# A mixture-of-experts kernel on one core: 71 half tiles a unit in place of 72

## The reference

```python
def moe(t, router, W1, b1, W2, b2):          # t: 4096 tokens x 128 channels, one image
    weight, index = top_k(softmax(layernorm(t) @ router), 2)
    h = gelu(einsum("nd,edf->enf", xn, W1) + b1)     # 128 -> 512
    y = einsum("enf,efd->end", h, W2) + b2           # 512 -> 128
    return t + einsum("ne,end->nd", combine(weight, index), y)
x = x + gated(ln(x));      x = x + moe(x, layer 0)    # both images
x = x + pools(ln(x));      x = x + moe(x, layer 1)    # max pools of 7 sizes, mixed
```

## Time and profile before

| | us |
|---|---|
| median of 3 runs | 1134.44 |
| lowest, highest | 1126.28, 1143.79 |
| the profiled execution | 1131.95 |
| its span, from the first to the last instruction | 1130.2 |
| busy in it: PE, POOL, DVE, ACT | 832.7, 620.7, 566.2, 522.3 |

### The profile page before, as it was taken

How to read it: one execution, slowest core, us unless ns; L and a number is a source line. 1 busy time by engine, 2 the same in 40 slices (tenths; PEclk the granted TensorE clock), 3 DMA queues, 4 the chain that set the end, 5 groups by cost and what they waited for, 6 DMA issues and landing times.

```text
span 1130.2 us, 14753 instructions
## 1 busy us (share of the span) xinstructions
PE 832.7 (74%) x4305; PEld 701.0 (62%) x4305; DVE 566.2 (50%) x1308; ACT 522.3 (46%) x1427; POOL 620.7 (55%) x598
## 2 busy tenths in 40 slices
PE   1854389888977777986787579976886877778780
PEld 1434267776776665865777467866776755657680
DVE  8957902280500292999883577999481003300004
ACT  1405045453454445653294256642483534444463
POOL 1000266766766655688634555788545665656651
PEclk9876579988988877998689598987797987879895
DMA  7001343443465752454157633533255645636356
GB/s 315 1 0 65 128 144 116 138 134 111 157 210 187 231 191 89 148 158 131 42 153 249 229 120 110 184 119 97 69 137 195 209 154 163 204 113 213 113 182 223
DMA packets 55391, 167.63 MB, mean 148 GB/s; under 512 B 13888, under 2 KB 13901, under 8 KB 55056
## 3 DMA queue, kind: packets, MB, share of 16 engines
q1 hardware_dynamic: 36880, 130.98, 34.7%
q0 software_dynamic: 18432, 35.70, 11.2%
HBM read 137.26 MB, written 31.46 MB: 149 GB/s over the span
## 4 chain that ended last, share of the span: by engine, by line
PE 43%; DVE 23%; ACT 11%; issue 9%; another core or an unknown queue 9%; DMA 2%; POOL 1%; SPq 0%; POOLq 0%; ACTq 0%; DVEq 0%
PE h_ps L773 15%; PE yT_ps L786 14%; DVE state L1292 5%; PE turn_ps L708 5%; ACT hT L586 4%; DVE work L1278 4%; DVE work L1273 4%; PE acc_ps L725 3%; PE acc_ps L745 2%; DVE work L1286 2%; PE xT_ps L762 2%; ACT yT L597 1%; ACT work L624 1%; PE yr_ps L796 1%
## 5 line engine op out<-in xcount | busy, mean ns | idle before, releaser
L501 POOL DMA_INDIRECT xg<-xn_rows,tile_rows x288 | 307.7, 1068 | 247.1 <-DVEq L1208 126.7
L510 POOL DMA_INDIRECT y_rows<-yr,tile_rows x288 | 308.8, 1072 | 238.6 <-ACT yr L606 157.2
L773 PE MATMUL h_ps<-xT,expert 128*128 128x256 f32 (+1 forms) x1408 | 327.3, 382 | 76.6 <-issue 40.9
L786 PE MATMUL yT_ps<-hT,expert 128*128 128x256 f32 (+1 forms) x1408 | 310.6, 373 | 40.8 <-ACT yT L597 37.3
L586 ACT ACTIVATE hT<-h_ps,expert 128x256 f32<-128x256 f32 (+1 forms) x704 | 254.6, 449 | 153.5 <-PE h_ps L773 62.9
L773 PEld LDWEIGHTS h_ps<-xT,expert 128*128 128x128 f32 x1408 | 250.3, 214 | 116.4 <-issue 75.0
L786 PEld LDWEIGHTS yT_ps<-hT,expert 128*128 128x128 f32 x1408 | 254.6, 212 | 80.6 <-ACT yT L597 45.2
L1242 DVE SCALAR_TENSOR_TENSOR tok<-work,share,tok 128x128 f32<-128x128 f32 x224 | 61.5, 345 | 343.4 <-DMA work<-y_rows 341.4
L597 ACT ACTIVATE yT<-yT_ps,expert 128x256 f32<-128x256 f32 (+1 forms) x176 | 74.1, 443 | 188.0 <-PE yT_ps L786 87.3
L574 ACT ACTIVATE xT<-xT_ps 128x256 f32<-128x256 f32 x144 | 56.4, 392 | 97.5 <-PE xT_ps L762 64.7
L762 PE MATMUL xT_ps<-ident,xg 128*128 128x128 f32 x288 | 61.7, 298 | 40.3 <-DMA xg<-xn_rows,tile_rows 32.8
(11 more groups left out here) (210 smaller groups left out, 644.3 us busy)
## 6 DMA issues: line engine op xcount, KB each, us to landing
expert<-in_experts SPq DMA_DIRECT2D x176, 514.5 KB
work<-y_rows SPq DMA_DIRECT2D x24, 512.0 KB
xn_rows<-work SPq DMA_DIRECT2D x16, 512.0 KB, 5.0
xg<-xn_rows,tile_rows POOLq DMA_INDIRECT x288
y_rows<-yr,tile_rows POOLq DMA_INDIRECT x288
tok<-in_x_tokens SPq DMA_DIRECT2D x8, 512.0 KB, 7.0
state<-in_x SPq DMA_DIRECT2D x2, 2048.0 KB, 17.4
work<-y_rows SPq DMA_DIRECT2D x16, 256.0 KB, 6.0
```

Of the source, the lines that this page charges most:

```text
L501: pool.indirect_dma_start(xg[:, s, h, :], None, xn_rows[unit], bass.IndirectOffsetOnAxis(ap=tile_rows[unit % 2][:, at, 0, h:h + 1], axis=0)) \
L510: pool.indirect_dma_start(y_rows[unit], bass.IndirectOffsetOnAxis(ap=tile_rows[unit % 2][:, at, 1, h:h + 1], axis=0), yr[:, s, h, :], None ...
L773: mm = pe.matmul(h_ps[c // 2][:, c % 2, cols], expert[:, t.load(h) % W_RING, c * P:(c + 1) * P], xT[:, t.slot(2), cols], start=True, stop= ...
L786: mm = pe.matmul(yT_ps[:, cols], expert[:, t.load(h, d) % W_RING, HIDDEN + c * P:HIDDEN + (c + 1) * P], hT[:, s, c, cols], start=(c == 0), ...
```

## The change

The 72nd half tile is left out. A new constant `SEATS` = 71 counts the half tiles of a unit, and the last tile (tile 35) has one half in place of two. Its gather, `turn_x`, `turn_y` and scatter issue one instruction instead of two; its `up` and `down` have 4 matmuls of 128 columns each instead of 8; `activate` has four instructions instead of eight, and `copy_y` one instead of two. `copy_x` and `copy_rows` stay as they are, at 256 columns, and so do the tables of routing, which keep 72 columns, but for the list of experts, which has 43. `LOADS` is 43. `landed`, which gives the semaphore value to wait for, now leaves out the halves that the short tiles don't have.

```diff
-LOADS = FULL + SPLIT * HALVES
+SEATS = (PAIRS + EXPERTS * (P - 1)) // P
+LOADS = SEATS - FULL
...
-    def landed(self, d=0, each=1):
-        return ((self.s + d) // RING + 1) * 16 * each
+    def landed(self, d=0):
+
+        at = self.s + d
+        short = sum(HALVES * TILES - SEATS for u in range(at // TILES + 1)
+                    if (u + 1) * TILES - 1 <= at and ((u + 1) * TILES - 1 - at) % RING == 0)
+        return ((at // RING + 1) * HALVES - short) * 16
+
+    def halves(self, d=0):
+
+        return min(HALVES, SEATS - HALVES * self.at(d)[1])
 
     def parts(self, d=0):
 
-        return HALVES if self.at(d)[1] >= FULL else 1
+        return self.halves(d) if self.at(d)[1] >= FULL else 1
...
     n = t.parts(d)
-    return [(h, slice(h * SLOTS // n, (h + 1) * SLOTS // n)) for h in range(n)]
+    size = t.halves(d) * P // n
+    return [(h, slice(h * size, (h + 1) * size)) for h in range(n)]
...
-                for h in range(HALVES):
+                for h in range(t.halves(d)):
                     pool.indirect_dma_start(xg[:, s, h, :], None, xn_rows[unit],
...
-                for h in range(HALVES):
+                for h in range(t.halves(d)):
                     pool.indirect_dma_start(y_rows[unit],
...
-                for h in range(HALVES):
+                for h in range(t.halves(d)):
                     mm = pe.transpose(xT_ps[:, h * P:(h + 1) * P], xg[:, t.slot(RING, d), h, :], ident[:])
...
-                for h in range(HALVES):
+                for h in range(t.halves(d)):
                     mm = pe.transpose(yr_ps[:, h, :], yT[:, s, h * P:(h + 1) * P], ident[:])
```

More of the change, by code:

```diff
@@ L426, in load_outputs @@
                     for d in range(RING):
-                        sp.wait_ge(s_scat[last.slot(RING, -d)], last.landed(-d, HALVES))
+                        sp.wait_ge(s_scat[last.slot(RING, -d)], last.landed(-d))
                     sp.wait_ge(s_buf, u + 1)
@@ L603, in copy_rows @@
                 if t.old(d - RING):
-                    act.wait_ge(s_scat[s], t.landed(d - RING, HALVES))
+                    act.wait_ge(s_scat[s], t.landed(d - RING))
                 act.wait_ge(s_yr_ps, t.done(d))
@@ L757, in turn_x @@
             def turn_x(t, d):
-                pe.wait_ge(s_gath[t.slot(RING, d)], t.landed(d, HALVES))
+                pe.wait_ge(s_gath[t.slot(RING, d)], t.landed(d))
                 if t.old(d - 1):
                     pe.wait_ge(s_xt_sb, t.done(d - 1))
-                for h in range(HALVES):
+                for h in range(t.halves(d)):
                     mm = pe.transpose(xT_ps[:, h * P:(h + 1) * P], xg[:, t.slot(RING, d), h, :], ident[:])
```

## The result

The changed kernel takes 1124.64 us (median of 11 runs, 1117.01 to 1131.13) against 1133.34 for the kernel before in the same runs. The ratio is 0.9906, 95% interval 0.9877 to 0.9936, so 10.7 us less (7.3 to 13.9); it leaves out slow runs, as one of 2616.73 us of the kernel before, and is not the ratio of the two medians, which lie 8.70 us apart. The profiled execution took 1124.27 us with a span of 1121.3 and a mean granted clock of 0.844, before 0.840.

The account below looks back on a forecast made before the run. Tiles set the pace (chain: PE 43%, DVE 23%, ACT 11%) except where DVE's pools do. Units 0 to 3 save 2.87 + 1.28 + 3.04 + 2.37 = 9.56 us; 1134.44 - 9.56 = 1124.9 us, range 1112 to 1138.

Parts of the forecast that it names:

- the forecast case: Whole kernel: the saving of 9.56 us comes as summed, 1124.9 us, within 1118 to 1132; chance 0.56.
- Waits that hold the pace: Ends of units 0 to 2: ACT's late signals come unchanged, only the last scatter is saved, 1133.2 us; chance 0.22.
- Waits that go: Ends of units: the waits behind tile 35 vanish and all upper bounds hold, 1109.9 us; chance 0.12.
- unknown waits: ACT's waits for unexplained semaphores ahead of `copy_y` and `activate`, 142.3 us; a change above the sum would refute the forecast.
- The clock: Ends of units 0 to 2: longer PE waits lower the granted clock, costing 31.1 us, so 1156.0 us; chance 0.08.
- the prediction's estimate: Whole span: a granted clock lower by 0.01 costs about 10 us, over 832.7 us of PE's work.
- PE's halves: Tile 35 of units 0, 2 and 3: half of `up` and `down` and transposes save 2.87, 3.04 and 1.09 us.
- The end of unit 3: Last `up` and transpose save 1.09 us, one scatter less in POOL's queue 1.28 us, together 2.37 us.
- Loads: Four removed loads of 514.5 KB cost nothing, as SP waits for free buffers, not transfers; 1.4 us each where DMA is full.
- The step that failed: POOL's queue: four removed gathers save nothing; scatters save one pitch of 1.28 us at each of units 1 and 3.
- The range: Whole kernel: 1112 to 1138 us, leaving out the far ends of the last two rival cases.
- a second sum: Two removed scatters on the path, priced as whole transfers of 2.15 us each, would make the saving 1.7 us larger.

Follow-up runs that it names:

- the run with the work alone: Kernel before without PE's and ACT's work on each unit's 72nd half tile, loads, gathers and scatters kept: ratio 0.9936, -7.3 us (-11.2 to -3.3).
- the 28 left out: The change minus 14 gathers and 14 scatters (second halves, tiles 28 to 34, units 2 and 3): ratio 0.9683, 24 ± 11 us under the change.
- the 28 thin DMAs: The change with 14 gathers and 14 scatters in units 2 and 3 moving 8 KB in place of 64 KB each: ratio 0.9896, 11.8 us under before.

## Why the prediction was right, and where not

**The total and the forecast case.** 1124.9 us was forecast and 1124.64 measured. That they agree within 0.3 us is luck: the median of the kernel before moved by 1.10 us between the two sets of runs, and one term of the sum was too small, as said below. Waits that hold the pace (1133.2) are excluded by the interval of the change and by the run with the work alone. Waits that go (1109.9) did not occur: 137.8 us of unknown waits are left of 142.3, a change of 4.5, less than the sum. At unit 2 the 3.53 us of the earlier trace rows ahead of `activate` are gone, but 3.48 us now stand ahead of the same tile's `copy_y`, and at unit 0 5.13 us ahead of tile 34's. The clock (1156.0) did not fall: 0.844 against 0.840, and 0.848 against 0.844 in the runs of the change taken again. Of a fall with less work there is a sign in the run with fourteen halves of work left out (0.72 against 0.82 in one stretch, 0.833 against 0.844 over the span). The small rise, by the prediction's estimate up to 4 us, was in no term of the sum; no run tells what of the gain is the clock's.

**PE's halves.** 2.87 + 3.04 + 1.09 = 7.0 us, measured alone 7.3 (3.3 to 11.2). The term holds as a total; the two places with rows in the profile gave 0.90 and, by the point where one stops, 5.57 or 2.40, so the division among units is not shown. The end of unit 3 came as worked out, 2.17 of 2.37 us with five scatters 1.28 us apart.

**Loads.** Costed at nothing; four gave 0.7 ± 4.4 and fourteen -1.2 ± 5.0 us.

**The step that failed.** "The four removed gathers stand five tiles ahead of their use, and POOL has 238.6 us of idle time before scatters, most of it waiting for ACT" put four gathers and two scatters at nothing, and only two scatters, 2.56 us, in the sum. Measured, the eight transfers alone give 9.5 us (5.2 to 13.9), and by the 28 left out together 0.86 us each, two thirds of a pitch, which is 6.9 us for eight. The distance of five tiles says how late one gather may come; it says nothing of a queue that is itself among the busiest. The 238.6 us of the earlier trace rows contain 81.3 of "issue", which is part of every DMA's pitch. In a stretch of the kernel before where only tiles run, POOL's timeline reads, with the first and the last of eight DMAs and the next one:

```profile
330.43 1.01 POOL L510 DMA_INDIRECT y_rows<-yr,tile_rows  x1 [3.13 <-ACT yr L606]
...
339.52 0.97 POOL L501 DMA_INDIRECT xg<-xn_rows,tile_rows  x1 [0.30 <-issue]
343.70 1.00 POOL L510 DMA_INDIRECT y_rows<-yr,tile_rows  x1 [3.20 <-ACT yr L606]
```

From 330.43 to 340.49 us eight DMAs follow each other without a stop, then POOL stands 3.20 us for ACT and starts again at 343.70. So it is taken for three quarters of the time there, not all of it. A DMA less shortens such a run by 1.28 us, unless another wait takes its place; what the measured price adds is that most of it is not taken back.

**Why the sum came out all the same.** 7.3 + 6.9 = 14.2 us by the measured prices, and 9.56 in the sum; the change's 11.9 ± 2.8 holds both, the first near its upper end and the second near its lower. The range was wide enough for the missing 4 us.

**What the price of two removed scatters came to.** The prediction gave a second sum, 1.7 us larger, with a whole transfer's 2.15 us for each of them. That price lies above what was measured: the five scatters at the end of unit 3 stand 1.28 us apart, and each of the 28 left out gave 0.86 ± 0.4 us. The fit of the Trainium skill (DMA: Bandwidth & Descriptors, Anatomy of one DMA, SWDGE path), a fixed 2.0 us and bytes at 436 GB/s, makes a transfer of 8 KB an estimate of 2.02 us. The runs agree that bytes hardly count, 0.1 ± 5.2 us for the 28 thin DMAs together.

**What stays open.** ACT's unexplained waits. They do not shrink with 28 fewer indirect DMAs (131.3 us) or with thinner ones (156.8), so the length of POOL's runs is not their cause alone. And through which single wait a shorter POOL queue reaches the end is shown only at the end of unit 1, where the chain runs along it; elsewhere the price is measured, not followed. How much of it comes by way of the granted clock is open too. Why gathers behind the scatters cost 10 us was read from one list of waits and not tried further.

## What to carry to other kernels

Count a software queue's time as busy plus its issue gaps before calling it idle: here the 71% of POOL stood in the page as 55%, the chain gave it 2%, and its DMAs were worth two thirds of their pitch each. A prefetch distance hides latency, not throughput: a gather five tiles ahead still takes its turn in the queue, here 0.95 ± 0.6 us of it. When a change removes the same unit of work from several queues, leave each part out by itself, and then many at once: four halves told only that the transfers mattered, fourteen gave the price.

## What the hardware showed that I had not expected

An indirect DMA of 128 rows occupies POOL for about 1.0 us and the next starts 1.3 us after it, with 64 KB as with 8 KB. In a stretch where 28% of PE's records were left out, the granted clock was 0.72 in place of 0.82, and PE's busy time 11% less; over the span the runs had a mean of 0.833, the kernel before beside them 0.844. With 28 indirect DMAs less and all of PE's work kept it was 0.853. And swapping gathers and scatters in POOL's queue, with nothing added, took back 10.2 ± 4.4 of the 11.9 us that the change had won.
